# A gate's last 32 inner columns: four computed copies, or one spread through memory

## The reference, cut to what matters

```python
xn = layernorm(x)                                     # (4, 1024, 256)
b_a = x_last - xn                                     # x_last: xn one token earlier
h = tanh((xn + b_a * miu_x) @ A)                      # 5 sets of 32 codes
miu = einsum(h, Bp) + lam
w_in, k_in, v_in, r_in, g_in = xn + b_a * miu         # five mixtures
w = td_miu + tanh(w_in @ tdA) @ tdB
k, v, r = k_in @ Wk.T * exp(min(w, 0)), v_in @ Wv.T, r_in @ Wr.T
g = tanh(g_in @ Wg1) @ Wg2                            # Wg1: 256 x 160, Wg2: 160 x 256
y = wkv6(r, k, v, w, u)                               # recurrence over tokens, 4 heads of 64
attn = (groupnorm(y) * gamma + beta) * g @ Wo.T
ffn = relu(xn @ W1[e] + b1[e]) @ W2[e] + b2[e]        # e: each token's best of 8 experts, times its probability
out = x + attn + ffn
```

## Time and profile before

| | |
|---|---|
| median of 3 runs | 590.93 us (588.99 to 593.19) |
| span of the profiled execution, first to last instruction | 589.1 us |
| TensorE busy in it | 538.6 us, 91% |
| VectorE, ScalarE, GpSimd busy | 449.0, 340.0, 197.6 us |
| DMA: moved, share of 16 engines by SyncE's and GpSimd's queues | 60.75 MB, 26.8% and 16.3% |

### The profile page before, as it was taken

One profiled execution on the slowest core, in us unless ns is written; L12 is line 12 of the kernel. 1 busy time (PEld: TensorE's weight loads), 2 busy tenths in 40 slices (PEclk: granted clock), 3 DMA queues, 4 the chain that ended last, 5 costly groups with the idle time before them and its releaser, 6 DMA issues. The chain is left out here.

```text
span 589.1 us, 18805 instructions
## 1 busy us (share of the span) xinstructions
PE 538.6 (91%) x7278; PEld 483.6 (82%) x7278; DVE 449.0 (76%) x1116; ACT 340.0 (58%) x753; POOL 197.6 (34%) x156
## 2 busy tenths in 40 slices
PE   2779797988999999999999899999999999989984
PEld 2568587867899999999999789998999999979873
DVE  6879999875859596868688686959686868778552
ACT  4975563333575756566665556575656566555651
POOL 7901010130324434435244232533343424322333
PEclk9999898997999999999999999999999999999998
DMA  8989644779241434324333224143433433221223
GB/s 276 264 295 305 175 121 100 215 246 297 55 76 35 97 46 91 56 73 73 73 53 93 39 59 70 39 90 47 99 47 79 68 73 60 43 41 34 37 38 45
DMA packets 49802, 60.75 MB, mean 103 GB/s; under 512 B 5057, under 2 KB 44098, under 8 KB 49570
## 3 DMA queue, kind: packets, MB, share of 16 engines
q1 hardware_dynamic: 36898, 44.72, 26.8%
q0 software_dynamic: 11840, 14.42, 16.3%
q10 hardware_dynamic: 976, 0.41, 0.2%
HBM read 40.79 MB, written 23.07 MB: 108 GB/s over the span
## 5 line engine op out<-in xcount | busy, mean ns | idle before, releaser
L1738 POOL DMA_INDIRECT out<-rows,dst_row x39 | 65.4, 1678 | 214.2 <-DVE rows L1149 203.8
L1020 DVE SCALAR_TENSOR_TENSOR mix<-G,vec,ba 128x256 f32<-128x256 f32 x160 | 69.6, 477 | 15.2 <-PE G L435 15.1
L657 PE MATMUL F<-xsT,w1s 128*128 128x128 f32 x624 | 76.7, 276 | 1.8 <-issue 1.8
L657 PEld LDWEIGHTS F<-xsT,w1s 128*128 128x128 f32 x624 | 74.8, 192 | 3.7 <-issue 2.0
L665 PE MATMUL F<-w,hsT 128*128 x312 | 74.9, 383 | 0.3 <-ACT hsT L1538 0.3
L1538 ACT ACTIVATE hsT<-F,b1c 128x128 f32<-128x128 f32 x156 | 44.5, 369 | 35.7 <-PE F L657 29.2
L665 PEld LDWEIGHTS F<-w,hsT 128*128 128x128 f32 x312 | 57.2, 190 | 8.5 <-issue 0.5
L1059 DVE COPY_PREDICATED AP_<-msk,LL 128x256 f32<-128x256 uint32 x96 | 51.2, 534 | 16.3 <-issue 11.0
L1081 DVE TENSOR_TENSOR RK<-RK,D 128x256 f32<-128x256 f32 x112 | 47.2, 422 | 18.9 <-issue 10.2
L1028 DVE TENSOR_TENSOR mix<-mix,xnT 128x512 f32<-128x512 f32 x80 | 55.1, 689 | 1.5
L1724 POOL DMA_INDIRECT rows<-xn_d,src_row x39 | 40.6, 1042 | 39.1 <-PE F L646 22.2
(11 more groups left out here) (181 smaller groups left out, 1223.6 us busy)
## 6 DMA issues: line engine op xcount, KB each, us to landing
cd<-cd_d SPq DMA_DIRECT2D x30, 320.0 KB, 5.3
w<-in_W SPq DMA_DIRECT2D x16, 512.0 KB, 8.5
cd_d<-w SPq DMA_DIRECT2D x32, 160.0 KB, 2.9
b2t<-in_b SPq DMA_DIRECT2D x39, 128.0 KB
w<-in_x SPq DMA_DIRECT2D x8, 512.0 KB, 9.5
xn_d<-w SPq DMA_DIRECT2D x8, 512.0 KB
out<-in_x SPq DMA_DIRECT2D x8, 512.0 KB, 5.9
out<-res POOLq DMA_DIRECT2D x16, 256.0 KB, 4.7
```

What stands on the lines that cost most here:

```text
L657: i1 = pe.matmul(FB[:, k * P:(k + 1) * P], w1s[:, cc, k, :], xsT[:, cc, :], start=(cc == 0), stop=(cc == 1))
L1020: i1 = dve.scalar_tensor_tensor(mixed_in(u, c, n, cc), bk[:, cc * UN:(cc + 1) * UN], cvec(LAM + CC * n, cc), ba[:, cc, :, :].rearrange("p ...
L1738: pool.indirect_dma_start(io["out"], bass.IndirectOffsetOnAxis(dst_row[:, f:f + 1], 0), ys[:, f % 2, :], None, compute_op=ALU.add).then_in ...
```

## The change

The rest of 32 inner columns is computed once for each token. `gate_down` puts the four quarters of the unit's tokens (`QT = 64`) on the four partition groups: eight matmuls of 32 output columns and 64 moving columns with a tile position of their own, ahead of the two wide ones. The bank holds 320 columns instead of 512. ScalarE's tanh covers 320 columns and its copy 64, into `ghl[:, u, 0]`; VectorE's `gate_terms` subtracts on 64 columns into `ghl[:, u, 1]`. From there SyncE writes both parts to a buffer in memory, `gd_d`, by four DMAs of 16 KB (`keep_gate`), and reads them back by two DMAs of 64 KB into the two halves of `tgx`'s partitions (`gate`), so that the four groups hold rounded part and difference of all 256 tokens. `gate_up` waits for `tg` and for these reads (`gr0`, `gr1`). Wg1 is no longer padded.

```diff
--- before.py
+++ after.py
@@ -81,6 +81,8 @@
 ROWS = NB * (T + 1) + PAD
 CSN, CRN = 64, 32
+GDN, GRN = 64, 32
+QT = UN // 4
 def seq(u, c):
@@ -112,7 +114,7 @@
         tdB = sb("tdB", [UB * TDR, C])
         wk, wr, wv, wo = (sb(n, [P, CC, C]) for n in ("wk", "wr", "wv", "wo"))
-        wg1 = sb("wg1", [P, CC, 2 * P])
+        wg1 = sb("wg1", [P, CC, GR])
         wg2x = sb("wg2x", [P, C], F32R)
         wg2 = sb("wg2", [P, C])
         vec = sb("vec", [P, NVEC])
@@ -142,7 +144,8 @@
         D = sb("D", [P, 2, 2 * CC * UN])
         V = sb("V", [P, 2, UB, C])
-        tg = sb("tg", [P, 2, 2 * UN])
+        tg = sb("tg", [P, 2, UN + QT])
+        ghl = sb("ghl", [P, 2, 2, QT])
         tgx = sb("tgx", [P, 2, UN], F32R)
         tw = sb("tw", [UB * TDR, P])
         AT = sb("AT", [P, 2, H2, CC, UB, P])
@@ -493,9 +495,12 @@
                 pe.wait_ge(s["x"], nth(u, c, 4))
                 pe.wait_ge(s["m"], nth(u, c, 4))
                 bk = bank(u, c, "tg")
-                for k in range(2):
-                    for cc in range(CC):
-                        i1 = pe.matmul(bk[:, k * UN:(k + 1) * UN], wg1[:, cc, k * P:(k + 1) * P], mixed_in(u, c, 4, cc), start=(cc == 0), stop=(cc == 1))
+                for cc in range(CC):
+                    for t in range(4):
+                        pe.matmul(bk[LORA * t:LORA * (t + 1), UN:UN + QT], wg1[:, cc, P:GR], mixed_in(u, c, 4, cc)[:, QT * t:QT * (t + 1)],
+                                  start=(cc == 0), stop=(cc == 1), tile_position=(0, LORA * t))
+                for cc in range(CC):
+                    i1 = pe.matmul(bk[:, 0:UN], wg1[:, cc, 0:P], mixed_in(u, c, 4, cc), start=(cc == 0), stop=(cc == 1))
                 i1.then_inc(s["gm"])
             def first_levels(u, c):
@@ -605,7 +610,8 @@
             def gate_up(u, c):
                 q = seq(u, c)
-                pe.wait_ge(s["tx"], q + 1)
+                pe.wait_ge(s["tg"], q + 1)
+                pe.wait_ge(s[f"gr{u}"], GRN * (c + 1))
                 if not q:
                     pe.wait_ge(s["gx"], 2)
                 if c < NCH - 1:
@@ -1138,8 +1144,7 @@
             def gate_terms(u, c):
                 dve.wait_ge(s["th"], seq(u, c) + 1)
-                rest = tg[:, u, UN:2 * UN]
-                dve.scalar_tensor_tensor(tgx[:, u, :], tgh, con[:, LOW:LOW + 1], rest, ALU.mult, ALU.add).then_inc(s["tx"])
+                dve.tensor_tensor(ghl[:, u, 1, :].bitcast(F32R), tg[:, u, UN:UN + QT], ghl[:, u, 0, :], ALU.subtract).then_inc(s["tx"])
             def expert_out(f):
                 dve.wait_ge(s["fym"], f + 1)
@@ -1435,11 +1440,11 @@
                 act.wait_ge(s["gm"], q + 1)
                 if q > 1:
                     act.wait_ge(s["gg"], q - 1)
-                act.activation(tg[:, u, :], bank(u, c, "tg")[:, :], ACT.Tanh).then_inc(s["tg"])
+                act.activation(tg[:, u, :], bank(u, c, "tg")[:, 0:UN + QT], ACT.Tanh).then_inc(s["tg"])
                 act.wait_ge(s["tg"], q + 1)
-                if q:
-                    act.wait_ge(s["tx"], q)
-                act.activation(tgh.bitcast(F32R), tg[:, u, UN:2 * UN], ACT.Copy).then_inc(s["th"])
+                if c:
+                    act.wait_ge(s[f"gd{u}"], GDN * c)
+                act.activation(ghl[:, u, 0, :].bitcast(F32R), tg[:, u, UN:UN + QT], ACT.Copy).then_inc(s["th"])
             def bonus(u, c):
                 q = seq(u, c)
@@ -1817,6 +1822,22 @@
                     sp.dma_start(cd[2 * LORA * k:2 * LORA * (k + 1), u, :, :].rearrange("r s (b n) -> r s b n", b=UB),
                                  src[:, :, UB * u:UB * (u + 1), :]).then_inc(s[f"cr{u}"], 16)
+            def keep_gate(u, c):
+                sp.wait_ge(s["th"], seq(u, c) + 1)
+                sp.wait_ge(s["tx"], seq(u, c) + 1)
+                if c:
+                    sp.wait_ge(s[f"gr{u}"], GRN * c)
+                own = gd_d[2 * LORA * u:2 * LORA * (u + 1), :]
+                for t in range(4):
+                    sp.dma_start(own[:, QT * t:QT * (t + 1)].rearrange("(x r) n -> r x n", x=2), ghl[LORA * t:LORA * (t + 1), u, :, :]).then_inc(s[f"gd{u}"], 16)
+
+            def gate(u, c):
+                sp.wait_ge(s[f"gd{u}"], GDN * (c + 1))
+                if c:
+                    sp.wait_ge(s["gg"], seq(u, c) - 1)
+                for k in range(2):
+                    sp.dma_start(tgx[2 * LORA * k:2 * LORA * (k + 1), u, :].bitcast(F32), gd_d[2 * LORA * u:2 * LORA * (u + 1), :]).then_inc(s[f"gr{u}"], 16)
+
             def out_is_x(k):
                 if k < NCH:
                     at = slice(NB * P * k, NB * P * (k + 1))
@@ -1834,9 +1855,11 @@
                 u, c = h % 2, h // 2
                 if c + 1 + u < NCH:
                     codes(1 - u, c + 1 + u)
+                keep_gate(*other(u, c))
                 for f in tiles_of(h):
                     if f is not None:
                         bias(f + 1)
+                gate(*other(u, c))
             for j in range(NJ):
                 load(j)
@@ -1876,7 +1899,13 @@
                 keep_codes(c)
                 if c + 3 <= NCH:
                     out_is_x(c + 3)
+                if c == 5:
+                    keep_gate(0, 0)
+                elif c == 6:
+                    gate(0, 0)
+                    keep_gate(1, 0)
             keep_codes(NCH - 1)
+            gate(1, 0)
             codes(1, 1)
             for k in range(3):
                 sp.wait_ge(s[f"ck{k}"], CSN * ((NCH + 2 - k) // 3))
@@ -1892,6 +1921,8 @@
                              io["W2"][e].rearrange("(c p) n -> p c n", p=P)).then_inc(s["ew2"], 16)
             for h in range(1, NU - 2):
                 half(h)
+            keep_gate(1, NCH - 1)
+            gate(1, NCH - 1)
             for f in LAST[1:]:
                 bias(f)
             sp.wait_ge(s["out"], 16 * (NCH + 1))
```

More of the change, by code:

```diff
@@ L179, in program @@
         cd_d = nc.dram_tensor("cd_d", [NCH * 2 * LORA, NSEG * P], F32, kind="Internal").ap()
+        gd_d = nc.dram_tensor("gd_d", [2 * 2 * LORA, UN], F32, kind="Internal").ap()
         s = {n: ctx.enter_context(nc.semaphore("s_" + n)) for n in (
@@ L189, in program @@
             "cr0 cr1 "
-            "ba mm m x tA tw tB d km k vm v rm r gm tg th tx gx "
+            "ba mm m x tA tw tB d km k vm v rm r gm tg th tx gx gd0 gd1 gr0 gr1 "
             "ru lev a gr sv big spread "
@@ L217, in program @@
         ident = con[:, IDN:IDN + P]
-        tgh = con[:, TRI:TRI + UN]
         rsv = Ru[:, :, :, :, :].rearrange("p c b k n -> p (c b k n)")[:, 0:COLS].rearrange("p (x g n) -> p x g n", x=2, n=LEAF // 2)
@@ L1946 @@
         "WkT": g["a_Wk"].T, "WvT": g["a_Wv"].T, "WrT": g["a_Wr"].T, "WoT": g["a_Wo"].T,
-        "Wg1": four(g["a_Wg1"], 1), "Wg2": four(g["a_Wg2"], 0), "Wr": np.pad(g["f_Wr"], ((0, 0), (0, LORA - E))), "br": g["f_br"].reshape(E),
+        "Wg1": g["a_Wg1"], "Wg2": four(g["a_Wg2"], 0), "Wr": np.pad(g["f_Wr"], ((0, 0), (0, LORA - E))), "br": g["f_br"].reshape(E),
         "W1": g["f_W1"], "W2": g["f_W2"], "b1c": g["f_b1"].reshape(E * HC, P).T, "b2": g["f_b2"].reshape(E * C),
```

## The result

| | before | changed |
|---|---|---|
| median of 16 runs each, us | 591.80 (587.44 to 593.19) | 588.07 (585.34 to 590.48) |
| ratio, 95% interval | | 0.9943 (0.9925 to 0.9961) |
| span of the profiled execution, us | 589.1 | 588.0 |
| mean granted clock in it | 0.982 | 0.974 |
| TensorE, VectorE, ScalarE busy, us | 538.6, 449.0, 340.0 | 537.6, 445.0, 335.2 |

The change saves 0.57%, some 3.4 us of 590.93, where I forecast 8.3. The kernel became faster, and 588.07 us lies inside the whole range of 578.5 to 589.5, but outside the 580.5 to 585 that I gave the forecast itself.

What follows compares the result with a forecast made beforehand. TensorE bounds the kernel from about 160 to 545 us. TensorE's 6.9 plus VectorE's 1.35 make 8.3 us: 590.93 - 8.3 = 582.6 us, own range 580.5 to 585, whole range 578.5 to 589.5.

Steps and rivals of the forecast that it cites:

- the price of the new part: In gate_down on TensorE: eight small matmuls cost 0.28 us plus 0.09 for going over to tiles, gain 0.495 a call.
- On the way back I see no cost: TensorE after gate_down's small matmuls: returning from tiled to untiled work costs nothing; only the way in costs 0.09 us.
- My bound: Worst case for gate_down's new part: 37.5 ns per instruction and the changeover twice, 0.60 + 0.18 = 0.78 us, gain 0.09.
- Rival 1: gate_down's small matmuls have a fixed spacing of 29 ns whatever their columns: gain 0.315 a call, 585.2 us; chance 0.17.
- Rival 2: gate_down's small matmuls run two groups at a time, 37.5 ns each, with both changeovers: 588.4 us; chance 0.11.
- rival 4: Slower: gate_down's four column groups don't overlap, 98 ns per instruction, 599.4 us; chance 0.06, shared with any other costly new stall.
- The short halves: Halves 1, 7 and 13, with two expert tiles: shorter gate_terms on VectorE saves 3 x 0.27 = 0.8 us.
- The 0.54 of the startup: Shorter gate_terms on VectorE counts twice before 99.29 us, where TensorE waits for VectorE's shifted codes: 0.54 us.
- ScalarE and the tail: ScalarE's shorter tanh and copy count nothing; at the end the later bias load comes out even, up to 1 us for the range.
- The bias load itself: In the tail it goes out near 556 us, behind the new DMAs; ScalarE uses it at 559.76: even, counted as nothing.
- the six DMAs, the codes, gate_up: SyncE's extra DMAs per half stay hidden: codes slide 1.2 us, gate_up's reads have 15 us of slack; no cost.
- rival 5: Low-clock stretches at 1.2 GHz vanish or repeat with the new timing: 4 us less or more, 578.6 or 586.6; chance 0.05.

Runs made afterwards that it cites:

- the repetition: The kernel before and the changed kernel measured again on one chip, differing from the first ones only by a remark: 588.42 and 580.67 us, ratio 0.9844.
- the second comparison: The changed kernel, unchanged, against the kernel before, both measured again on another chip: 580.67 beside 588.42 us, ratio 0.9844.

## Why the prediction was wrong, point by point

**The step that failed** is the price of the new part, 0.28 + 0.09 = 0.37 us, and in it the sentence "On the way back I see no cost". The instructions were dear enough in my estimate (17.5 ns; 14.4 measured). The way in was right (0.09). But the way back costs 0.12 + 0.11 us. So the part costs 0.55, a call gains 0.31 instead of 0.495, and 14 calls 4.3 us instead of 6.9. My bound allowed a changeover twice, 0.18 us; the real one is 0.32. The trace of before already had a row for the way back. The middle levels are three groups of 32 equal matmuls; the first two take 0.49 and 0.46 us, and the third, which a product of the whole array follows, takes 249.75 - 249.17 = 0.58:

```profile
249.17 0.65 PE L525 MATMUL LL<-RK 64*64 64x32 f32 x32
249.75 0.50 PE L435 MATMUL G<-cd,bst 128*128 128x256 f32 x2
```

**Rival 1** gave this size (0.315 a call) from another mechanism, a fixed 29 ns for each small matmul. The doubled rest refutes it. Rival 2's 37.5 ns and rival 4's 98 ns fall with it: four groups of 64 columns do overlap.

**The short halves** (0.8 us) are the second step that failed. I took TensorE's wait for VectorE as VectorE being late by its own work. Both wait there in turn, and gate_terms lies in VectorE's part of the idle time: 0 us. The 0.54 of the startup was right (0.25 or 0.26 for each of two, at like clocks).

**ScalarE and the tail.** I counted nothing. The tail became 0.68 us shorter, 0.65 in the repetition. GpSimd in the tail, before:

```profile
549.29 1.59 POOL L1738 DMA_INDIRECT out<-rows,dst_row  x1 [7.82 <-DVE rows L1149]
555.53 1.31 POOL L1744 DMA_DIRECT2D out<-res  x1 [4.65 <-DMA out<-rows,dst_row]
556.34 2.22 POOL L1716 TENSOR_TENSOR gn<-gn,small 128x8 f32<-128x8 f32 x1
```

and changed:

```profile
547.64 1.59 POOL L1743 DMA_INDIRECT out<-rows,dst_row  x1 [7.52 <-DVE rows L1154]
552.14 1.31 POOL L1749 DMA_DIRECT2D out<-res  x1 [2.91 <-DMA out<-rows,dst_row]
554.32 1.67 POOL L1721 TENSOR_TENSOR gn<-gn,small 128x8 f32<-128x8 f32 x1 [0.87 <-DVE gn L1122]
```

A scatter, then a store that waits for it, then the group norm's step, which VectorE and through it TensorE's `hidden` wait for. The store goes out 6.2 us after the scatter before and 4.5 us after it now, so gn no longer waits for GpSimd but for VectorE. With the trip for chunk 0 alone, whose bias load isn't held back, it is 4.8 us, and the tail as short as in the changed kernel (33.83 against 33.84 us): the later bias load isn't the reason, and what is stays open. The bias load itself was as harmless as forecast: ScalarE's row at 558.08 waits 0.18 us, as at 559.76 before.

**Hidden, as forecast:** the six DMAs, the codes, gate_up. **The sum with the measured terms** is 4.3 + 0.5 + 0.65 = 5.5 us instead of 8.3, beside the 4.1 us and the estimate of 5.5 by which the pair differs at equal clock. Between this sum and the 3.4 us of the first comparison stand, in its two traces, the standstill of 1.24 us and 3.4 us more lost to the clock; how often its other runs had them no record shows.

**The clock** (rival 5) I gave 0.05, as something that the change might move once. It is rather a scatter between executions that both kernels have: 7 to 15 us lost, on average, over the runs of one kernel on one chip. Of the 8.1 us of the second comparison it is an estimated 2.6. The traces don't show that the change moves it. The clocks of the first comparison's runs of before aren't on record, so for that one it isn't worked out. That the median lies inside the whole range is owed to the range's width, which rivals 1 and 2 had widened, and not to the sum.

## What to carry to other kernels

Cutting wide matmuls into a few that share the array's column groups cost 14 ns an instruction here, but 0.3 us for going in and out; put next to work that is tiled already, 0.19 of that is saved, of which 0.10 a period arrived. The kernel with the small ones behind the levels does that: 578.39 us against 580.67 and 588.78 on one chip. Of the 2.3 us below the changed kernel the rows explain 13 x 0.10 = 1.3, and the runs of the two overlap. And where engine A waits for B, look whether B waits for A just before: work taken off B in that idle time is worth nothing.

## What the runs showed of the hardware

- A crossing between whole-array and column-group matmuls costs 0.1 us in the row of the whole-array work beside it (0.09 to 0.11 in four places), and there the next weight load starts with its matmul and not 0.1 us ahead. The end of a tiled group takes 0.12 us more, ahead of the whole array and ahead of another tile shape.
- Four column groups of 32 with 64 moving columns in float32 run at 14.4 ns per instruction.
- TensorE stood still for 0.6 to 1.85 us, between groups or in the middle of one, up to three times in a profiled execution, with and without the trip's DMAs. All nine cases end 2.3 to 2.9 us after a 16 KB packet of the instruction queue starts.
- The startup's stretches at 1.2 GHz differ between executions of the same kernel (one window of 4 us or four from 128 to 144 us), and with them that stretch's length (34.83 or 39.16 us). The long ones follow three gaps of 0.4 us in TensorE's work.
